# Cross-attention layer: attention stage from f32r pairs to scaled f16 pairs, and the first query tile's mask added by TensorE

## The chip, the cores and the metric

The kernel runs on one core of a Trainium2 chip. The metric is the device time of one execution in microseconds. In the views PE is TensorE (PEld its weight loads), DVE VectorE, ACT ScalarE, POOL GpSimd, and SP the engine that issues most DMAs.

## The reference

A transformer layer over 16 sequences of 512 tokens and 512 features: cross attention with 16 heads of 32, queries from `x`, keys and values from a context, then a feed-forward block of 2048.

```python
q, k, v = heads(query @ Wq + bq), heads(key @ Wk + bk), heads(values @ Wv + bv)
scores = einsum('bhqd,bhkd->bhqk', q, k) / sqrt(32)
scores = where(j < i, scores, -1e30)            # strictly causal
attn = softmax(scores); attn[:, :, 0, :] = 0
x = layer_norm(query + (attn @ v) @ Wo + bo, g1, b1_)
out = layer_norm(x + relu(x @ W1 + b1) @ W2 + b2, g2, b2_)
```

Inputs, weights and the result are f32, and the result has to keep nearly f32 accuracy. So every operand of TensorE is held as a high part and a low part (the rest), and each product is made of three matmuls: high by high, high by low, low by high.

## The kernel before

There are two stages: attention over 16 items (the sequences), and feed over 32 chunks of 256 tokens (output projection, both norms, the feed-forward block in f16 pairs). Attention writes its heads' outputs to memory (`ctx_rows`), feed reads them.

**Slots.** Each engine's program is a loop over windows, each of 48 slots. `due(window, slot, SLOTS, items, first, span)` says which items have their step `first + k` in this slot; a step number over 47 belongs to the next windows, so three items are in work at once. Within a slot each engine does what is due in the order in which it is written, and waits on semaphores for the others. All step numbers are constants at the top of `attention`. `side_by_side` mixes feed's program into attention's from slot 48 x 16 + `FEED_AFTER` on, one step of feed to two slots.

**Steps of an item.** Pieces of the context and of x (four each, 128 x 512) are loaded into the one buffer `raw` (`CTX_LOAD` 14, `X_LOAD` 27), split by ACT (high part, f32r, L459) and DVE (low part, L524) into `acts`. From `LIN` = 32 on, PE makes 12 projection units (`UNITS`: four of v, and k and q for each of four head groups), each of four slots with three matmuls (L720, L724). Of a v unit ACT and DVE take three bf16 parts out of PSUM: L476, L644 (rest into `vf`), L481, L649. Of a k or q unit they take a high and a low f32r part into `stage` (L491, L658). When a group's q is staged, SP issues 12 DMAs (`heads_moves`, L360) that lay its heads' high and low parts out as 96 rows in `heads`; each moves 128 KB.
From `MAX_AT` = 57 on, one group in 12 slots, PE makes the scores for the row maxima (L699, 11 units of a group, `MAX_UNITS`), into two banks of `max_ps`; DVE adds the mask and takes the maximum in one pass for each head (L678). The negated maxima, two parts, are transposed (L629) and moved by SP into rows 96 and 97 of `heads` (L398, four DMAs). From `ST_AT` = 74 on PE makes the transposed scores with the maximum subtracted (L746) and adds masks by a matmul with an identity (L781); ACT takes two exponentials (f32 and f16, L514, L516), POOL the low part (L435), and PE multiplies with V three slots later (L766 high, 97 columns; L768 low, 65). DVE sums the three parts of V (L599), inverts the row sum (L602) and scales (L610); SP stores the group (L389, L390).
PE in slot s may start a unit of max scores when DVE has read the unit two slots before (`max_read`).

**Beside it.** Each item also loads a piece of W1 or W2 into `raw`, and DVE looks for its largest magnitude (L582); for W2 POOL mixes blocks (L451) and SP stores them (L337). From these bounds feed's f16 scales are made.

**Start and end.** At the start v's weights and the first context come in turn, and each piece is split as soon as it is there (`first_split`, L463 and L529). Where attention's last item drains, feed's weights are split into f16 pairs in memory that attention has left, each with a wait for what was there (`before.*`).

## Time and profile before

| | |
|---|---|
| median of three runs | 2659.24 us (2656.49 to 2664.09) |
| profiled execution, span | 2657.7 us (its own time outside the span is not given; the median is 1.5 us above) |
| busy share of PE, PEld, DVE, ACT, POOL | 98%, 84%, 79%, 58%, 60% |
| chain that ended last, by engine | PE 87%, DVE 4%, SP's queue 2%, POOL 2%, DMA 2%, ACT 1% |
| DMA | 273.35 MB, mean 103 GB/s; `heads<-stage` 748 issues of 128 KB |

Shares of busy time are averages over both stages. A matmul's duration holds its way through the array, and consecutive ones overlap, so their rate is read from start to start. A time of a group by form is the mean of one instruction; starts of back-to-back DVE instructions lie somewhat closer.

### The profile page before, as it was taken

The page shows a single profiled execution, that of the slowest core. Times are in us where ns is not written, and L with a number is a line of the kernel's source. Part 1 is how long each engine was busy: PE and PEld are TensorE (multiplying, and loading weights), DVE is VectorE, ACT ScalarE, POOL GpSimd, SP SyncE. Part 2 cuts the span into 40 slices and gives each one's busy share as a digit, 9 for nine tenths or more (in the row PEclk, how much of TensorE's full clock was granted, in tenths as well). Part 3 has the DMA queues.
Part 4 walks back from the last instruction along what each step waited for, and adds up shares of the span by engine and source line. Part 5 has one row for each costly group of instructions (what it writes and reads, how often), then busy time and mean ns, then how long its engine had stood idle before and what let it go on. Part 6 is the DMA issues. An engine that isn't in the chain of part 4 may idle for free.

```text
span 2657.7 us, 62252 instructions
## 1 busy us (share of the span) xinstructions
PE 2605.2 (98%) x22600; PEld 2245.5 (84%) x22600; DVE 2088.3 (79%) x5171; ACT 1530.3 (58%) x2945; POOL 1587.9 (60%) x1721
## 2 busy tenths in 40 slices
PE   7999999999999999988999999999999999999998
PEld 5888888888888888867888888888888888888887
DVE  6888988888888888888767766676767676767675
ACT  4777877787777777766343434343434344444433
POOL 3777777766666666666555555454555555555543
PEclk9999999999999999989999999999999999999999
DMA  6566655565556555656131323222222222222220
GB/s 189 154 154 163 157 152 155 145 166 143 143 145 152 144 142 138 147 140 171 48 67 47 70 50 69 52 66 55 59 62 56 64 57 64 57 65 57 64 55 27
DMA packets 439556, 273.35 MB, mean 103 GB/s; under 512 B 299648, under 2 KB 334400, under 8 KB 439248
## 3 DMA queue, kind: packets, MB, share of 16 engines
q1 hardware_dynamic: 437648, 266.74, 40.3%
q10 hardware_dynamic: 1600, 2.62, 0.5%
q8 instruction: 178, 2.92, 0.5%
q14 instruction: 130, 1.06, 0.1%
HBM read 109.86 MB, written 57.67 MB: 63 GB/s over the span
## 4 chain that ended last, share of the span: by engine, by line
PE 87%; DVE 4%; SPq 2%; issue 2%; POOL 2%; DMA 2%; ACT 1%; ACTq 0%; DVEq 0%; POOLq 0%
PE h_ps L1443 23%; PE acc L1459 20%; PE lin_ps L724 12%; PE lin_ps L720 6%; PE front L1429 6%; PE max_ps L699 6%; PE st_ps L746 6%; PE o_ps L766 4%; PE o_ps L768 3%; PE st_ps L781 2%; POOL prob_lo L435 1%; SPq L866 1%; SPq L360 1%; DVE W L1400 1%; DMA x_in<-in_x 0%
## 5 line engine op out<-in xcount | busy, mean ns | idle before, releaser
L435 POOL TENSOR_TENSOR prob_lo<-probs,prob_hi 128x512 f16<-128x512 f32 (+1 forms) x768 | 785.1, 1035 | 369.2 <-ACT prob_hi L516 365.1
L1443 PE MATMUL h_ps<-x_halves,W 128*128 128x256 f16 x6144 | 757.2, 273 | 3.1 <-ACT hf L1234 1.7
L1443 PEld LDWEIGHTS h_ps<-x_halves,W 128*128 128x128 f16 x6144 | 596.9, 98 | 89.6 <-issue 12.0
L1459 PE MATMUL acc<-W,hs 128*128 128x256 f16 x5376 | 669.6, 273 | 0.0
L1234 ACT ACTIVATE hf<-h_ps,b1s,scale_evac 128x256 f32<-128x256 f32 x512 | 284.7, 562 | 530.5 <-PE h_ps L1443 530.1
L678 DVE CUSTOM_DVE_ANT_0 max_ps<-max_ps,mask_q 128x128 f32<-128x128 f32 (+3 forms) x1024 | 486.2, 506 | 123.6 <-PE max_ps L699 107.6
L1459 PEld LDWEIGHTS acc<-W,hs 128*128 128x128 f16 x5376 | 526.0, 98 | 60.8
L514 ACT ACTIVATE probs<-st_ps 128x512 f32<-128x512 f32 (+1 forms) x768 | 406.4, 529 | 240.5 <-PE st_ps L781 221.2
L1158 POOL TENSOR_TENSOR hf<-hf 128x256 f32<-128x256 f32 x256 | 248.5, 971 | 462.1 <-ACT hf L1234 462.0
L1396 DVE TENSOR_TENSOR hs<-hf,hs 128x896 f16<-128x896 f32 x256 | 286.9, 1141 | 157.4 <-ACT hs L1223 157.3
L516 ACT ACTIVATE prob_hi<-st_ps 128x512 f16<-128x512 f32 (+1 forms) x768 | 406.7, 530 | 0.0
L1223 ACT ACTIVATE hs<-hf 128x896 f16<-128x896 f32 x256 | 242.2, 946 | 272.6 <-POOL hf L1161 269.4
L746 PE MATMUL st_ps<-heads 98*128 98x512 f32 (+3 forms) x1024 | 310.1, 344 | 2.3 <-DMA heads<-rows 2.1
L699 PE MATMUL max_ps<-heads 96*128 96x128 f32 (+3 forms) x1024 | 279.7, 325 | 8.5 <-DVE maxima L678 6.9
L766 PE MATMUL o_ps<-V,prob_hi 128*128 128x97 bf16 x2560 | 242.9, 208 | 9.8 <-DVE onorm L610 8.5
L1159 POOL TENSOR_TENSOR hf<-hf 128x256 f32<-128x256 f32 x256 | 237.7, 929 | 0.0
L768 PE MATMUL o_ps<-V,prob_lo 128*128 128x65 bf16 x2560 | 237.5, 193 | 0.0
L720 PE MATMUL lin_ps<-wv,ctxT 128*128 128x512 f32 x768 | 226.8, 406 | 6.4 <-DVE ctxT L529 6.4
L699 PEld LDWEIGHTS max_ps<-heads 96*128 96x128 f32 x1024 | 184.8, 191 | 56.9 <-DVE maxima L678 15.9
L724 PE MATMUL lin_ps<-xT,wq 128*128 128x512 f32 x768 | 227.3, 405 | 3.4 <-DVE vf L644 2.6
L724 PE MATMUL lin_ps<-ctxT,wk 128*128 128x512 f32 x768 | 220.2, 396 | 0.0
L766 PEld LDWEIGHTS o_ps<-V,prob_hi 128*128 128x128 f16 x2560 | 210.2, 98 | 11.1 <-DVE onorm L610 9.9
(121 smaller groups left out, 3797.4 us busy)
## 6 DMA issues: line engine op xcount, KB each, us to landing
heads<-stage SPq DMA_DIRECT2D x748, 128.0 KB, 2.6
raw<-in_xT SPq DMA_DIRECT2D x64, 256.0 KB, 3.0
o_in<-ctx_rows SPq DMA_DIRECT2D x256, 64.0 KB, 2.6
x_in<-in_x SPq DMA_DIRECT2D x32, 512.0 KB, 4.1
x_rows<-x SPq DMA_DIRECT2D x64, 256.0 KB, 2.0
o_in<-x_rows SPq DMA_DIRECT2D x256, 64.0 KB, 2.4
out<-y SPq DMA_DIRECT2D x32, 512.0 KB, 3.1
raw<-in_cT SPq DMA_DIRECT2D x60, 256.0 KB, 3.5
```

The lines of the kernel that those rows point to most:

```text
L435: pool.tensor_tensor(prob_lo[:, k % 4, 0:w], probs[:, k % PROBS, 0:w], prob_hi[:, k % 4, 0:w], ALU.subtract).then_inc(pl_done, 1)
L514: act.activation(probs[:, k % PROBS, 0:w], st_ps[:, k % 2, 0:w], ACT.Exp, bias=PROB_BIAS, scale=SCALE)
L516: act.activation(prob_hi[:, k % 4, 0:w], st_ps[:, k % 2, 0:w], ACT.Exp, bias=PROB_BIAS, scale=SCALE).then_inc(exp_done, 1)
L678: last = dve.tensor_tensor_reduce(out=scores[:, a, :], in0=scores[:, a, :], in1=mask, scale=1.0, scalar=MASKED, op0=ALU.add, op1=ALU.max, ...
L699: last = pe.matmul(max_ps[:, bank, a * w:(a + 1) * w], heads[0:96, t, 0, i, q * P:(q + 1) * P], heads[0:96, t, 1, i, 0:w], start=(a == 0), ...
L720: last = pe.matmul(lin_ps[:, n % 2, :], a[:, aw, j, t * P:(t + 1) * P], W[kind][:, aa, j, :], start=(j == 0 and m == 0), stop=(j == KT - 1 ...
L724: last = pe.matmul(lin_ps[:, n % 2, :], W[kind][:, aw, j, t * P:(t + 1) * P], a[:, aa, j, :], start=(j == 0 and m == 0), stop=(j == KT - 1 ...
L746: last = pe.matmul(st_ps[:, k % 2, at:at + w], heads[0:98, t, 1, i, kt * P:(kt + 1) * P], heads[0:98, t, 0, i, kt * P:S], start=(opens and ...
L766: pe.matmul(o[:, 0:3 * HD + 1], prob_hi[:, k % 4, col:col + P], v[:, 0:3 * HD + 1], start=(k % 3 == 0 and q == 0), stop=False, skip_group_ ...
L768: last = pe.matmul(o[:, HD:3 * HD + 1], prob_lo[:, k % 4, col:col + P], v[:, HD:3 * HD + 1], start=False, stop=(c == 2), skip_group_check= ...
L1443: last = pe.matmul(h_ps[:, f % 2, 0:T], W1[:, aw, j, f * P:(f + 1) * P], x1_halves[:, item.parity, aa, j, :], start=(j == 0 and m == 0), s ...
L1459: last = pe.matmul(acc_products[:, n, :], hs[:, p % HS, aa, n, :], W2[:, p, aw, n, :], start=(p == 0 and m == 0 and n % 2 == 0), stop=(p = ...
```

## The change

All of attention's TensorE operands become pairs of f16, as in feed. f16 has a small range, so each operand is multiplied by a power of two that the kernel finds on the chip. For every item DVE looks at both halves of c and of x for the largest magnitude per partition (four reductions over 1024 elements), joins them, SP writes them to memory (`SPREAD`) and reads them back into every partition (`GATHER`), and DVE makes from them the exponent, its inverse, the scaled biases, the exponential's scale and the values' scale (`ranges`, `RANGE`). The splits multiply by the inverse. The weights and the first item get the same at the start (`first_look`, `first_join`, `first_ranges`), in two groups: c, v and k first, then x and q; no weight and no piece is split before its group's range is known. V has two f16 parts in place of three bf16 parts. The raw pieces of c, of x and of the scanned weights get buffers of their own, and `acts` becomes double. In the max scores of the first query tile the mask is added by a fifth matmul, and DVE takes one reduction over all four heads. Steps move: `LIN` from 32 to 40 and all that hangs on it, loads and splits too, `FEED_AFTER` from 30 to 38. The places in memory are laid out anew, and with them the waits of feed for what attention leaves.

```diff
+    LOAD = {"c": 0, "x": 8}
+    LOOK = {"c": 5, "x": 13}
+    TOPS = 16
+    SPREAD = 17
+    GATHER = 20
+    RANGE = 24
+    SPLIT = {"c": 28, "x": 40}
+    SPLIT_STEP = 3
+    LIN = 40
...
+        acts = sb("acts", [P, 2, 2, 2, KT, S], F16)
+        raw = {"c": sb("raw_c", [P, KT, S], F32), "x": sb("raw_x", [P, KT, S], F32)}
+        W = {w: sb(f"w{w}", [P, 2, KT, D], F16) for w in WEIGHTS}
+        stage = sb("stage", [P, 2, 2, 2, S], F16)
+        scan = sb("scan", [P, KT, D], F32)
+        heads_at = sb("heads", [P, GROUPS, 2, 4, S], F16)
...
+        V = sb("V", [P, 2, QT, HEADS, VW], F16)
...
+                for kind in KINDS:
+                    for j in range(KT):
+                        for item, _ in after_first(due(window, s, SLOTS, B, LOAD[kind] + j)):
+                            wait_for(sp, lo_done, NCHUNK, item, chunk_of(kind, j) + 1 - NCHUNK)
+                            load(kind, item, j)
...
+                for item, _ in after_first(due(window, s, SLOTS, B, SPREAD)):
+                    wait_for(sp, top_ready, 1, item, 0)
+                    sp.dma_start(top_rows, top[:, :]).then_inc(top_spread, 16)
+                for item, _ in after_first(due(window, s, SLOTS, B, GATHER)):
+                    wait_for(sp, top_spread, 16, item, 0)
+                    wait_for(sp, range_step, RANGE_STEPS, item, 1 - 2 * RANGE_STEPS)
+                    sp.dma_start(gathered[:, 0:P, :].rearrange("p r k -> p (r k)"),
+                                 top_rows.rearrange("p k -> (p k)").rearrange("(a n) -> a n", a=1)
+                                 .to_broadcast([P, 2 * P])).then_inc(top_gathered, 16)
...
+            wait_for(act, raw_loaded[kind][j], 16, item, 16)
+            act.wait_ge(*ranged(item, 3))
+            act.activation(act_part(item, kind, 0)[:, j, :], raw[kind][:, j, :], ACT.Copy,
+                           scale=inverse[:, item.n % 3, KINDS.index(kind):KINDS.index(kind) + 1]).then_inc(hi_done, 1)
...
+            dve.scalar_tensor_tensor(out=act_part(item, kind, 1)[:, j, :], in0=raw[kind][:, j, :],
+                                     scalar=inverse[:, item.n % 3, i:i + 1], in1=act_part(item, kind, 0)[:, j, :],
+                                     op0=ALU.mult, op1=ALU.subtract).then_inc(lo_done, 1)
...
+                            for j in (2 * half, 2 * half + 1):
+                                wait_for(dve, raw_loaded[kind][j], 16, item, 16)
+                            wait_for(dve, top_ready, 1, item, -1)
+                            dve.tensor_reduce(top_parts[:, KINDS.index(kind), half:half + 1],
+                                              raw[kind][:, 2 * half:2 * half + 2, :].rearrange("p i n -> p (i n)"),
+                                              AX_X, ALU.max, apply_absolute_value=True).then_inc(top_seen, 1)
...
+            wait_for(dve, top_gathered, 16, item, 0)
+            dve.tensor_reduce(tops[:, :], gathered[:, :, :].rearrange("p r k -> p k r"), AX_X, ALU.max
+                              ).then_inc(range_step, 1)
+            dve.tensor_scalar(power[:, at, :].bitcast(U32), tops[:, :].bitcast(U32), EXPONENT, None, ALU.bitwise_and
+                              ).then_inc(range_step, 1)
+            dve.reciprocal(inverse[:, at, :], power[:, at, :]).then_inc(range_step, 1)
...
+        first_join(0, 7)
+        for half in range(2):
+            first_look(1, 0, half, raw_loaded["x"][2 * half:2 * half + 2], raw["x"])
+            first_look(1, 1, half, first_loaded["q"][2 * half:2 * half + 2], first[:, 2, :, :])
+        first_ranges(0)
+        first_join(1, 5)
+        for w, j in FIRST_TURN:
+            if w == "c":
+                split(Item(0), "c", j)
+            else:
+                split_weight(w, j)
+        first_ranges(1)
...
+                            dve.tensor_tensor(V[:, item.parity, t, :, 0:HD],
+                                              lin_ps[:, n % 2, :].rearrange("p (h d) -> p h d", d=HD),
+                                              V[:, item.parity, t, :, HD:2 * HD], ALU.subtract
+                                              ).then_inc(lin_out, 1)
...
-                                          o[:, :, 0:3 * HD].rearrange("p q (c d) -> p q d c", c=3),
+                                          o[:, :, 0:2 * HD].rearrange("p q (c d) -> p q d c", c=2),
...
+                            if q == 0:
+                                dve.tensor_reduce(maxima[:, t % 2, 0, :], scores, AX_X, ALU.max
+                                                  ).then_inc(max_read, 1)
+                                continue
...
+            if q == 0:
+                last = pe.matmul(max_ps[:, bank, :].rearrange("p (h n) -> p h n", n=P), identb[:, :],
+                                 mask_q0[:, :].unsqueeze(1).to_broadcast([P, 4, P]), start=False, stop=True,
...
-                        pe.matmul(o[:, 0:3 * HD + 1], prob_hi[:, k % 4, col:col + P], v[:, 0:3 * HD + 1],
+                        pe.matmul(o[:, 0:2 * HD + 1], prob_hi[:, k % 4, col:col + P], v[:, 0:2 * HD + 1],
...
-                        last = pe.matmul(o[:, HD:3 * HD + 1], prob_lo[:, k % 4, col:col + P],
-                                         v[:, HD:3 * HD + 1], start=False, stop=(c == 2),
+                        last = pe.matmul(o[:, HD:2 * HD + 1], prob_lo[:, k % 4, col:col + P],
+                                         v[:, HD:2 * HD + 1], start=False, stop=(c == 2),
```

## Rows read from the trace of the kernel before

**Rows 1.** Busy time by window: stretch, length, engines' busy us (instructions), clock, DMA share, GB/s.

```profile
300.00:1000.00 700.00, 698.98 (x6346) 593.00 (x6345) 621.77 (x2117) 554.32 (x1191) 497.69 (x496) 1.00 0.59 149
...
1150.00:1200.00 50.00, 40.91 (x317) 32.43 (x317) 44.52 (x99) 36.05 (x73) 32.87 (x29) 0.90 0.44 120
...
1400.00:2600.00 1200.00, 1199.90 (x10265) 1054.09 (x10264) 859.38 (x1400) 498.44 (x805) 640.45 (x750) 1.00 0.26 59
```

**Rows 2.** Waits, 300 to 1000 us: total us, times, longest.

```profile
DVE max_ps L678 <- PE max_ps L699: 64.5, 128, 1.7
...
PEld max_ps L699 <- DVE maxima L678: 4.8, 11, 0.5
```

**Rows 3.** Groups by form, 300 to 1000 us, PE projections: busy us, mean ns, idle.

```profile
L720 PE MATMUL lin_ps<-wv,ctxT 128*128 128x512 f32 x480 | 139.9, 399 | 0.0
```

**Rows 4.** PE in order of time: start us, us, instruction.

```profile
640.63 0.21 PE L766 MATMUL o_ps<-V,prob_hi 128*128 128x97 bf16 x1
640.68 0.19 PE L768 MATMUL o_ps<-V,prob_lo 128*128 128x65 bf16 x1
640.71 0.21 PE L766 MATMUL o_ps<-V,prob_hi 128*128 128x97 bf16 x1
...
641.23 0.27 PE L781 MATMUL st_ps<-mask_k,identb 128*128 128x256 bf16 x1
```

**Rows 5.** Chain of waits, 1090 to 1260 us: start us, us, what.

```profile
1122.55 0.70 PE lin_ps L724 x3
...
1254.63 1.31 PE acc L1459 x12
```

**Rows 6.** Groups by form, 300 to 1000 us, weight loads.

```profile
L766 PEld LDWEIGHTS o_ps<-V,prob_hi 128*128 128x128 f16 x1586 | 129.0, 97 | 0.1
...
L699 PEld LDWEIGHTS max_ps<-heads 96*128 96x128 f32 x633 | 113.2, 189 | 29.2 <-DVE maxima L678 4.8
```

**Rows 7.** Groups by form, 300 to 1000 us, DVE.

```profile
L599 DVE TENSOR_REDUCE osum<-o_ps 128x128 f32<-128x384 f32 x159 | 87.7, 552 | 0.0
...
L649 DVE TENSOR_TENSOR V<-vf,V 128x512 bf16<-128x512 f32 x40 | 41.1, 1028 | 0.0
...
L524 DVE TENSOR_TENSOR xT<-raw,xT 128x512 fp32r<-128x512 f32 x40 | 36.9, 922 | 0.0
...
L582 DVE TENSOR_REDUCE scan_part<-raw 128x1 f32<-128x1024 f32 x10 | 12.1, 1214 | 0.0
...
L588 DVE TENSOR_TENSOR scan_top<-scan_top,scan_part 128x1 f32<-128x1 f32 x10 | 1.9, 189 | 0.3
```

**Rows 8.** Groups by form, 1400 to 2600 us, DVE.

```profile
L1321 DVE SCALAR_TENSOR_TENSOR x_halves<-block_turned,scale,x_halves 128x512 f16<-128x512 f32 x54 | 53.4, 988 | 61.5 <-ACT x_halves L1187 61.5
```

**Rows 9.** DVE in order of time, first query tile of a group.

```profile
651.92 0.30 DVE L678 CUSTOM_DVE_ANT_0 max_ps<-max_ps,mask_q 128x128 f32<-128x128 f32 x1
...
652.91 0.44 DVE L678 CUSTOM_DVE_ANT_0 max_ps<-max_ps,mask_q 128x256 f32<-128x256 f32 x1
```

**Rows 10.** SP's queue in order of time.

```profile
618.03 2.66 SPq L398 DMA_DIRECT2D heads<-rows  x4
...
636.24 0.41 SPq L350 DMA_DIRECT2D raw<-in_xT  x1
636.75 7.85 SPq L360 DMA_DIRECT2D heads<-stage  x12
```

**Rows 11.** DMA issues, 300 to 1000 us: count, KB, median us to landing.

```profile
raw<-in_xT SPq DMA_DIRECT2D x40, 256.0 KB, 3.0
```

**Rows 12.** Busy time by window, at the start.

```profile
4.00:8.00 4.00, 2.25 (x5) 1.38 (x6) 2.77 (x4) 2.31 (x4) 4.00 (x1) 1.00 0.97 354
```

**Rows 13.** All engines in order of time, at the start.

```profile
4.03 0.69 DVE L529 TENSOR_TENSOR wv<-first,wv 128x512 fp32r<-128x512 f32 x1 [4.03 <-ACT wv L463]
...
13.70 0.68 DVE L644 TENSOR_TENSOR vf<-lin_ps,V 128x512 f32<-128x512 f32 x1
```

549 lines of the change are left out of this document (337 added, 212 removed).

## The prediction

> **What bounds the kernel now.** I read the windows by stage first, then who waits for whom, then groups by form, then single stretches in order of time. The windows [rows 1] show two stages. In 300 to 1000 us, the middle of the attention stage, PE is busy for 698.98 of 700 us at the full granted clock, DVE for 621.77, ACT 554.32, POOL 497.69. In 1400 to 2600 us, the feed stage, PE is busy 1199.90 of 1200 us. Between them, at 1150 to 1200 us, PE leaves 9 of 50 us idle and its granted clock is 0.90. The waits of the attention stretch [rows 2] run one way: DVE waits 64.5 us for PE's max scores, PE waits 4.8 us for DVE. So PE sets the pace, and the question is who is second. 480 value matmuls fall in the 700 us [rows 3] and a sequence has 48 of them: one sequence takes 70.0 us. In these 70.0 us DVE works 62.2, ACT 55.4, POOL 49.8. DVE has 7.8 us of slack, and that is all that a faster PE can win before DVE binds.
>
> **PE, per sequence.** In order of time [rows 4] the 16 value matmuls from 640.63 to the mask at 641.23 take 0.60 us, so a pair (97 and 65 columns) takes 75 ns: from the first to the second 0.05, back 0.03. Three projection matmuls of 512 columns take 0.70 us [rows 5], 233 ns each. A sequence has 144 projections (33.6 us) and 160 pairs (12.0 us). The rest, 24.4 us, is 64 max-score and 64 transposed-score matmuls (20480 columns each) and 48 masks (8192 columns).
> The rate of f16 operands stands in the feed stage: 12 matmuls of 256 columns in 1.31 us [rows 5], 109 ns each or 0.426 ns a column. At that rate the projections take 144 x 0.218 = 31.4 us (2.2 less), and the rest 49152 x 0.426 = 20.9 us (3.5 less). Value pairs get 65 and 33 columns. 65 is measured at 29 ns (to 30 as printed); 33 lies between its columns alone (14 ns) and the same 29. I take 29, since the fixed part of so short a matmul is not shown: 160 x 0.058 = 9.3 us, 2.7 less. The new mask matmul, 512 columns, comes four times: 0.9 us more. Sum 70.0 - 2.2 - 3.5 - 2.7 + 0.9 = 62.5 us. Lower end, with 14 ns for 33 columns: 60.1. Upper end, if the scores and masks gain nothing: 66.0.
> The Trainium skill, "TensorE: Matmul & The Clock Gate", section "Wait — 56ns, not 53.3ns?", gives a floor of about 25 ns from start to start for any short matmul. By it a pair would take 54 ns and the PE sum, as an estimate, 61.9; no row here has a matmul that short.
> Why f32 operands pay more: the weight loads take 189 ns in f32 and 97 in f16 [rows 6], the first not far from the 233 ns of a 512-column matmul beside which the next load has to pass.
>
> **DVE, per sequence** [rows 7 to 9]. Gone: the second value subtraction, L649, 41.1 us in ten sequences, 4.1. The first one (L644) stays as the only one, at its price. The three-way sum of L599 becomes two-way, 384 to 256 elements: from L582 (1024 elements, 1214 ns) and L599 (384, 552 ns) 128 elements cost 0.132 us, so 16 x 0.132 = 2.1. The first query tile's four mask-and-max steps take 0.99 us (651.92 to 652.91); one reduction over 512 elements costs 0.552 + 0.132 = 0.68: 4 x 0.31 = 1.2 less. Added: four looks over 1024 elements, one for each half of each input, 4 x 1.214 = 4.9; one small maximum and the range steps (a reduction over 258 elements 0.42, five small ones at about 0.2, as L588 takes 0.19) 1.6. The splits become a scaled subtraction with f16 out. The same form in the feed stage takes 988 ns [rows 8] against 922 now: 8 x 0.07 = 0.6 more (at best the 690 ns of the undisturbed start [rows 13], 1.9 less). Sum 62.2 - 4.1 - 2.1 - 1.2 + 6.5 + 0.6 = 61.9 us, bounds 59.4 and 63.
> The Trainium skill, "SBUF — State Buffer", section "Who interferes with whom", has it that a DVE instruction with two SBUF inputs and a GpSimd one that reads SBUF lock each other out, which fits 922 ns beside POOL's work and 690 before it began. The rule speaks against the hope that f16 makes the splits cheap: by it they stay two-input instructions, and the sum, as an estimate, stays within 0.6 us of mine.
> So DVE's load stays, and PE comes down to it: 62.5 against 61.9.
>
> **ACT and POOL.** ACT loses the third value piece (4 x about 0.6 us) and works 53. POOL keeps 49.8. Both stay below 62 and hide.
>
> **The new wait: loads behind the head moves on SP.** SP issues in program order. The moves of one head group are 12 DMAs, 7.85 us by the clock of the queue [rows 10], 0.65 each; a whole load takes 0.5 and a quartet of row moves 2.66. Halving the bytes need not shorten this, as a load of twice the bytes takes less time to issue. Per sequence SP issues 48 moves (31 us), 16 row moves (11), ten loads (5) and eight stores, which I put at 10: some 57 of 70 us. Two more small DMAs (the spread and the gather of the ranges) make 58; SP as a whole does not bind.
> The order does. The x loads stand at slots 8 to 11 and the moves of group 0 at slot 9, so pieces 2 and 3 are issued behind all 12. The moves wait for DVE's q piece of slot 8. From there 12 x 0.62 = 7.4, two issues 0.9 and 2.6 to 3.0 us to landing [rows 11] give 10.9 to 11.3 us, and 1.3 more in the first eight sequences, where the store of the mixed W2 stands between. DVE comes to the second x look (slot 15) after about 7 slots of 1.3 us with the first two x pieces in hand; its own work in them is some 7.5 us, PE's 8.5 to 9. So it waits about 2.5 us (ends 0 and 3.8). What is queued behind: DVE's whole slot 15 and all later ones, among them the max reads that free PE's two banks; PE may run two slots ahead, no more. With DVE and PE both near 62, this wait is not absorbed.
> Behind it hang the small maximum, the spread (SP, behind four row moves), 2 to 2.5 us to memory, the gather and again 2.5 us back, due on DVE at slot 24, 16 slots or 21.6 us after slot 8. The chain is 11.1 + 1.4 + 2.7 + 0.5 + 2.3 + 0.5 + 2.8 = 21.3 us: just in time. But SP stands still for the round trip at slot 20, and the group 1 moves (slot 21) start late by about a slot, against a margin of 8 slots (10.8 us) less 7.4 + 2.5 us (to landing, put a little below the load's 3.0). I put 0.7 us on both, with the unevenness of slots (ends 0 and 4).
> Sum of the new period: 61.9 + 0.4 for dependent small steps + 2.6 + 0.7 = 65.6 us, 4.4 less than now.
>
> **Start.** Now the first value piece leaves PSUM at 13.70 us [rows 13]. The change wants v, c, k and the biases looked at first. Twenty loads of 262 KB come in at 354 GB/s in 4 to 8 us and faster after [rows 12]: k is in by about 12 us, all by 17. DVE: four looks done by 11, biases and two k looks by 14.2; out to memory and back 0.5 + 2 + 0.5 + 2.5, to 19.7, with the x and q looks (4.9) beside it; 14 chained steps 3.3, to 23; eight splits of 0.69, to 28.7; the second range 3.3, to 32; the k splits 2.8, to 34.8. So 21 us later than now, nothing beside it on PE. Ends 14 and 27.
>
> **Between the stages.** The tail is paced by POOL, ACT and the feed stage's own weight splits, which keep their work; new places in memory drop a few waits for buffers and add others that are long over. I count 0, ends -8 and +6. The feed stage is untouched. The longer lead (40 slots for 32) holds no work and costs nothing.
>
> **Sum.** The pace of 70.0 us holds from 35 to 1110 us, 15.3 sequences: 15.3 x 4.4 = 67 us less; 21 more at the start: 46 less. The span of the profiled execution is 2657.7 us; 2611.7. The median of the runs is 1.5 us above that span, so 2613.
>
> **Rivals.**
> B, the look wait stays hidden: DVE's work between slots 8 and 15 is slower than I count, or the moves issue faster at half the bytes. Then PE's 62.5 sets the pace. For: raw loads issue in 0.5 us with twice the bytes; against: the moves' 0.65 us is steady whatever the traffic. 15.3 x 7.5 = 115 less, 21 more: 2565. Chance 0.25.
> C, SP's order takes the place of PE (the slower side): the x pieces late by 3.8 us with the mixed store, the ranges late at slot 24 by 1.5, the group 1 moves behind SP's standstill late by 2 at slot 29, on a DVE of 63. Period 70.3: 5 more and 21 more: 2685. It decides from a period of 68.6 on (15.3 x 1.4 = 21). For: SP is busy 57 of 70 us and waits now at DVE's q piece; against: all three must come in full. Chance 0.16.
> D, the change doesn't speed PE as it says: max and transposed scores keep their 24.4 us, as their time is in turn-around between differently shaped weights and not in f32. PE 66.0, with the looks partly beside it 67: 46 less, 21 more: 2634. For: 24.4 is 3.5 over the columns' 20.9 and I have f16 only in even streams; against: 189 ns loads. Chance 0.14.
> The forecast's own case, 2613, has 0.45, with 2590 to 2640 as its own range. Range over all: 2560 to 2662. A measurement tells 0.3%, 8 us, from no change: faster 0.79 (the forecast, B, most of D), same 0.06, slower 0.15.
>
> **What would show it.** Per sequence, by the count of value matmuls: 65.6 us; DVE busy over 92% of the stretch, PE near 95%, and PE's waits for DVE's max reads in tens of us where there were 4.8. The looks on x with a wait for a raw x load of 2 to 3 us, 15 times. Projections at 218 ns, value pairs at 58. First value piece out of PSUM near 35 us. Wrong: PE still busy 99.8% with a period near 62 (B), a wait of the PE for head moves (C), score matmuls at their old spacing (D), or a first value piece before 28 us.

## The result, and the profile after

| | before | after |
|---|---|---|
| median | 2658.74 us (2656.49 to 2664.09, four runs) | 2820.3 us (2815.91 to 2822.85, four runs) |
| ratio after/before, 95% interval | | 1.0605 [1.0589, 1.062] |
| span of the profiled execution | 2657.7 us | 2817.5 us |
| first value matmul of item 0 | 5.8 us | 27.2 us |
| from item 0's to item 1's | 59.5 us | 60.4 us |
| fourteen periods, items 1 to 15 | 988.1 us, 70.6 each | 1128.2 us, 80.6 each |
| from item 15's first value matmul to the end | 1604.3 us | 1601.7 us |

The change makes the kernel 6% slower, 207 us above the forecast of 2613 us. The last four rows are worked out from the trace: 48 projection matmuls of an item belong to the values, so the start of each 48th marks where an item begins on PE. They add up to the whole difference of the spans: 21.4 + 0.9 + 140.1 - 2.6 = 159.8 us. The start cost what was forecast (21.4 + 0.9, for 21), the passage between the stages about nothing (-2.6, for 0), and all of the miss lies in the period: 80.6 us where 65.6 was forecast. It isn't one number either. While the scan still mixes and stores W2 (items 1 to 7) a period is 81.8 to 84.1 us, afterwards 76.5 to 79.5.

Page of the kernel after, parts 1 and 4: busy time by engine, and the chain that ended last.

```profile
PE 2553.5 (91%) x22664; PEld 1903.7 (68%) x22664; DVE 2122.2 (75%) x4871; ACT 1628.7 (58%) x2881; POOL 1579.7 (56%) x1721
...
PE 53%; issue 11%; POOL 10%; DVE 10%; SPq 9%; DMA 6%; ACT 1%; POOLq 0%; DVEq 0%; ACTq 0%
```

The chain was 87% PE before. Now PE has 53% of it, nearly all in the feed stage, and the rest is spread over everything: issue, POOL, DVE, SP's queue, DMA. That is the picture of a loop in which no engine is full. The windows say the same (columns as in [rows 1]):

```profile
0.00:35.00 35.00, 7.85 (x23) 2.46 (x24) 24.05 (x55) 10.29 (x16) 12.16 (x20) 1.00 0.67 211
...
300.00:1000.00 700.00, 594.24 (x5613) 341.75 (x5613) 563.49 (x1686) 543.25 (x1013) 445.63 (x437) 0.94 0.35 93
...
1600.00:2700.00 1100.00, 1099.52 (x9402) 965.68 (x9400) 779.26 (x1278) 450.58 (x733) 567.85 (x688) 1.00 0.26 59
```

In the attention stretch PE is busy for 594 of 700 us where [rows 1] have 699, DVE for 563 where they have 622, and the granted clock is 0.94 where it was 1.00. The feed stage is as full as before. Times 80.6 and over 700 this is, per item: PE 68.4, DVE 64.9, ACT 62.6. None of them reaches 81.

The waits of the same stretch, a selection (total us, times, longest):

```profile
PE max_ps L905 <- DVE maxima L884: 70.7, 41, 7.5
DVE max_ps L884 <- PE max_ps L905: 63.1, 85, 1.8
PE o_ps L974 <- POOL prob_lo L493: 30.6, 40, 4.1
DVE top_parts L833 <- issue: 33.9, 5, 7.5
DVE top_parts L833 <- DMA raw_x<-in_xT: 12.3, 4, 3.4
DVE scan_part L772 <- DMA scan<-in_W: 11.0, 7, 2.1
POOL scan L508 <- DMA scan<-in_W: 20.6, 4, 5.5
DVE tops L678 <- DMA gathered<-top_rows: 4.4, 5, 2.1
```

In the kernel before, PE's weight loads waited 4.8 us for DVE's max reads [rows 2] and its matmuls not at all; the matmuls wait 70.7 us now. DVE's waits for the second x look are nine, 46.2 us by their two releasers: 5.9 to 7.5 us in each of five items, 2.4 to 3.4 in each of four later ones. Each is followed, 2 us on, by a wait of PE of the same length, which makes 46 of the 70.7 us. ("issue" here is a wait whose releaser, a DMA that landed long after it was issued, the view could not name; the timelines below show what it is.) So DVE waits for a load and PE for DVE. PE's 30.6 us for POOL's low parts have a like cause: while W2 is mixed, POOL stands for the scanned weights' load up to 5.5 us, and PE then 3.3 to 4.1 us for POOL, once an item.

One such stall in order of time. SP's queue:

```profile
445.61 0.89 SPq L352 DMA_DIRECT2D raw_x<-in_xT  x2
449.44 8.49 SPq L419 DMA_DIRECT2D heads<-stage  x12
457.98 0.58 SPq L352 DMA_DIRECT2D raw_x<-in_xT  x1
458.61 1.51 SPq L396 DMA_DIRECT2D mixed_w<-scan  x3
460.16 0.56 SPq L352 DMA_DIRECT2D raw_x<-in_xT  x1
...
467.64 2.68 SPq L456 DMA_DIRECT2D heads<-rows  x4
470.37 0.41 SPq L431 DMA_DIRECT2D top_rows<-top  x1
473.38 0.33 SPq L437 DMA_DIRECT2D gathered<-top_rows  x1
```

DVE and PE (start us, us, instruction):

```profile
455.24 1.19 DVE L833 TENSOR_REDUCE top_parts<-raw_x 128x1 f32<-128x1024 f32 x1
...
464.83 1.22 DVE L833 TENSOR_REDUCE top_parts<-raw_x 128x1 f32<-128x1024 f32 x1 [6.87 <-issue]
...
466.86 0.59 PE L905 MATMUL max_ps<-heads 96*128 96x128 f16 x4 [6.86 <-DVE maxima L884]
...
467.66 1.49 PE L932 MATMUL lin_ps<-acts,wq 128*128 128x512 f16 x3
...
470.42 0.81 PE L932 MATMUL lin_ps<-acts,wq 128*128 128x512 f16 x3
```

Windows across it:

```profile
461.00:463.00 2.00, 0.00 (x0) 0.00 (x0) 0.00 (x0) 0.00 (x0) 1.18 (x2) 1.00 1.09 396
463.00:465.00 2.00, 0.00 (x0) 0.00 (x0) 0.17 (x1) 0.00 (x0) 0.00 (x0) 0.55 0.29 108
465.00:467.00 2.00, 0.14 (x2) 0.17 (x3) 2.00 (x6) 0.00 (x0) 0.00 (x0) 0.50 0.37 114
467.00:469.00 2.00, 2.00 (x9) 0.88 (x8) 1.93 (x8) 0.00 (x0) 0.00 (x0) 0.50 0.04 11
469.00:471.00 2.00, 2.00 (x22) 1.40 (x21) 1.41 (x7) 1.07 (x3) 0.15 (x1) 0.75 0.03 3
```

The reader should follow one thing through these three views. The twelve moves of group 0 start when DVE's q piece is staged, at 449.4. Behind them SP issues a load, three stores of the mixed W2 and the last load, whose issue ends at 460.7 and which lands at 464.8, when the look starts. DVE came to the look at 458.0 and stood for 6.9 us; its max reads stood with it, PE stood for as long, and from 461 to 465 every engine but POOL is idle. PE then starts again at half the clock: the granted clock falls from 463 us on and is 0.50 at 465 to 469 us, the lower of its two levels (1.2 GHz), after PE has done nothing since 460. Three projection matmuls take 1.49 us there (at 467.66) and 0.81 us at 470.42, where the clock is back; from start to start it is 0.43 us for one against 0.22. The spread of the ranges stands behind the four row moves (2.7 us), and the gather is issued 3.0 us after the spread, as it waits for its landing: both as forecast.

What was forecast of PE's instructions came out. Value pairs and masks (columns as in [rows 4]):

```profile
477.61 0.19 PE L974 MATMUL o_ps<-V,prob_hi 128*128 128x65 f16 x1
477.64 0.18 PE L976 MATMUL o_ps<-V,prob_lo 128*128 128x33 f16 x1
...
477.94 0.22 PE L989 MATMUL st_ps<-mask_k,identb 128*128 128x128 bf16 x1
```

Six pairs in 0.33 us are 55 ns each (75 before). Starts of 512-column projections and scores lie 215 to 219 ns apart (projections 233 before), of 384 columns 165 to 166, of 256 columns 110 to 113 (medians). The mask matmul of 512 columns takes 220 ns. The Trainium skill, "TensorE: Matmul & The Clock Gate", section "Wait — 56ns, not 53.3ns?", has a floor of about 25 ns between starts; the 26 ns in which a 33-column matmul makes way for the next agree with it, where its columns alone would give 14.

Groups by form, 300 to 1000 us, a selection of those that answer to [rows 7 to 9] or are new:

```profile
L833 DVE TENSOR_REDUCE top_parts<-raw_x 128x1 f32<-128x1024 f32 x17 | 20.5, 1205 | 46.2 <-issue 33.9 <-DMA raw_x<-in_xT 12.3
L592 DVE SCALAR_TENSOR_TENSOR acts<-raw_c,inverse,acts 128x512 f16<-128x512 f32 x36 | 38.6, 1074 | 0.0
L804 DVE SCALAR_TENSOR_TENSOR onorm<-osum,value_scale,o_ps 128x128 f32<-128x128 f32 x139 | 47.4, 341 | 0.0
L790 DVE TENSOR_REDUCE osum<-o_ps 128x128 f32<-128x256 f32 x140 | 58.5, 418 | 0.0
L879 DVE TENSOR_REDUCE maxima<-max_ps 128x4 f32<-128x512 f32 x35 | 24.1, 688 | 3.1 <-PE max_ps L909 2.9 <-issue 0.2
L584 ACT ACTIVATE prob_hi<-st_ps,exp_scale 128x512 f16<-128x512 f32 x278 | 195.5, 703 | 0.0
```

The looks (1.21 forecast), the sum of two parts (0.42) and the one reduction (0.68) are at their forecast prices. Three are dearer: the splits at 1050 to 1074 ns for 988 forecast, the scaling at 341 for 280 before, and ACT's exponential at 703 ns for 598 before. The forecast had no term for the last two.

### The profile page after: what moved, and what is told of

Read it like the earlier page. It is cut to its first block, busy times and chain, and to the rows that moved or that the text cites. A ratio compares the mean times of both kernels' runs of the same rounds, so it can differ in the third digit from the quotient of the medians.

```text
span 2817.5 us, 62084 instructions
## 1 busy us (share of the span) xinstructions
PE 2553.5 (91%) x22664; PEld 1903.7 (68%) x22664; DVE 2122.2 (75%) x4871; ACT 1628.7 (58%) x2881; POOL 1579.7 (56%) x1721
## 3 DMA queue, kind: packets, MB, share of 16 engines
q14 instruction: 126, 1.03, 0.1%
## 4 chain that ended last, share of the span: by engine, by line
PE 53%; issue 11%; POOL 10%; DVE 10%; SPq 9%; DMA 6%; ACT 1%; POOLq 0%; DVEq 0%; ACTq 0%
PE h_ps L1649 22%; PE acc L1665 19%; POOL prob_lo L493 10%; SPq L419 7%; PE front L1635 6%; DVE max_ps L884 2%; PE lin_ps L932 2%; DMA scan<-in_W 1%; DMA raw_x<-in_xT 1%; DMA gathered<-top_rows 1%; SPq L456 1%; DMA top_rows<-top 1%; PE max_ps L905 1%; DVE W L1606 1%; PE st_ps L954 1%
## 5 line engine op out<-in xcount | busy, mean ns | idle before, releaser
L493 POOL TENSOR_TENSOR prob_lo<-probs,prob_hi 128x512 f16<-128x512 f32 (+1 forms) x768 | 793.3, 1043 | 461.1 <-ACT prob_hi L584 457.2
L1649 PEld LDWEIGHTS h_ps<-x_halves,W 128*128 128x128 f16 x6144 | 596.2, 98 | 90.7 <-issue 15.4
L582 ACT ACTIVATE probs<-st_ps,exp_scale 128x512 f32<-128x512 f32 (+1 forms) x768 | 482.8, 629 | 282.1 <-PE st_ps L989 231.4
L1665 PEld LDWEIGHTS acc<-W,hs 128*128 128x128 f16 x5376 | 525.9, 98 | 61.6 <-DVE hs L1602 0.8
L884 DVE CUSTOM_DVE_ANT_0 max_ps<-max_ps,mask_q 128x256 f32<-128x256 f32 (+2 forms) x768 | 420.1, 562 | 116.9 <-PE max_ps L905 115.6
L584 ACT ACTIVATE prob_hi<-st_ps,exp_scale 128x512 f16<-128x512 f32 (+1 forms) x768 | 484.1, 630 | 0.0
L905 PE MATMUL max_ps<-heads 96*128 96x128 f16 (+3 forms) x1024 | 267.0, 314 | 124.1 <-DVE maxima L884 116.0
L974 PE MATMUL o_ps<-V,prob_hi 128*128 128x65 f16 x2560 | 221.2, 193 | 77.0 <-POOL prob_lo L493 56.3
L954 PE MATMUL st_ps<-heads 98*128 98x512 f16 (+3 forms) x1024 | 275.1, 309 | 4.0 <-DMA heads<-rows 2.3
L928 PE MATMUL lin_ps<-wv,acts 128*128 128x512 f16 x768 | 211.3, 386 | 27.2 <-DVE acts L592 27.2
L932 PE MATMUL lin_ps<-acts,wq 128*128 128x512 f16 x768 | 225.9, 406 | 4.2 <-DVE V L851 4.2
L932 PE MATMUL lin_ps<-acts,wk 128*128 128x512 f16 x768 | 212.9, 387 | 3.1 <-DVE V L851 3.1
L976 PE MATMUL o_ps<-V,prob_lo 128*128 128x33 f16 x2560 | 213.1, 181 | 0.0
```

Of the source, the lines that this page charges most:

```text
L493: pool.tensor_tensor(prob_lo[:, k % 4, 0:w], probs[:, k % PROBS, 0:w], prob_hi[:, k % 4, 0:w], ALU.subtract).then_inc(pl_done, 1)
L582: act.activation(probs[:, k % PROBS, 0:w], st_ps[:, k % 2, 0:w], ACT.Exp, bias=PROB_BIAS, scale=exp_scale[:, at:at + 1])
L584: act.activation(prob_hi[:, k % 4, 0:w], st_ps[:, k % 2, 0:w], ACT.Exp, bias=PROB_BIAS, scale=exp_scale[:, at:at + 1]).then_inc(exp_done, 1)
L884: last = dve.tensor_tensor_reduce(out=scores[:, a, :], in0=scores[:, a, :], in1=mask_q[:, S - w:S], scale=1.0, scalar=MASKED, op0=ALU.add, ...
L905: last = pe.matmul(max_ps[:, bank, a * w:(a + 1) * w], heads[t][0:96, 0, i, q * P:(q + 1) * P], heads[t][0:96, 1, i, 0:w], start=(a == 0), ...
L932: last = pe.matmul(lin_ps[:, n % 2, :], W[kind][:, aw, j, t * P:(t + 1) * P], act_part(item, side, aa)[:, j, :], start=(j == 0 and m == 0) ...
```

## Experiments

A period is given as the mean of the fourteen from item 1 to item 15 (before: 70.6). E1 to E6 ask how much the wait for the loads and the search cost; E7 and E8 put parts of the f16 pairs alone into the kernel before; F and G, run afterwards, take the rest apart. The ratio is against runs of the kernel before on the same chip. The series ran on four chips, where the kernel before took 2659.5 (E1 to E4), 2657.6 (E5 to E8), 2657.9 (F) and 2657.6 us (G), so a difference of times between two series can be up to 2 us off.

**E1: the x loads before the head moves.** Only their place changes; the look, the moves and all else stay.

```diff
-    LOAD = {"c": 0, "x": 8}
+    LOAD = {"c": 0, "x": 4}
```

> The changed kernel with the x loads four slots earlier (slots 4 to 7), ahead of group 0's 12 head moves in SP's order; nothing else. Theory 1 (order): DVE's second x look waits 6.9 us (sequences with the mixed W2 store) or 3.4 us (those without) for x pieces issued behind the moves, and nothing absorbs it: the period falls from 82.5 and 78.5 us to about 76 and 75, the wait at the look goes to 0, and the time from 2820 to about 2740 us. Rival 2 (load): ACT at 62 us, DVE at 64 us per sequence and their uneven slots set the period; the wait only moves to another place: 2800 us or more.

Measured: 2775.1 us, 1.0439 [1.0423, 1.0455]. Windows, 300 to 1000 us:

```profile
300.00:1000.00 700.00, 609.01 (x5849) 350.03 (x5848) 603.85 (x1750) 564.02 (x1052) 461.63 (x454) 0.97 0.37 97
```

The waits of the x look are gone altogether, and with them 45 us. That lies between the expectation (about 2740) and its rival (2800 or more). So the mechanism was there, but it is not the main part: the periods are still 76.6 to 79.6, then 75.7 to 77.9, 77.4 in the mean. What is late next are the scan look (1 to 2 us) and the gather (up to 2.4 us).

**E2: the scan's load before the moves of group 3 as well.**

```diff
-    SCAN_LOAD = 42
+    SCAN_LOAD = 38
```

> As e1, and the scanned weights' load goes from slot 42 (behind the moves of group 3) to slot 38 (ahead of them). Theory 1: POOL's wait for this load (20.6 us in 8.75 sequences, four long ones of 5 us) and DVE's (1.4 to 2.1 us a sequence) go, and with them PE's waits for POOL's low parts (5 us a sequence in the first half): another 3 to 5 us a sequence in the first half and 1 in the second, 2740 to about 2705 us. Rival 2: no change against e1.

Measured: 2751.2 us, 1.0338 [1.0317, 1.0358]; period 75.8. The scan's load is worth 24 us, not the 35 expected. The order of loads is worth 69 us together (2820 to 2751), and 92 of the 161 us over before remain. The waits left in 300 to 1000 us, a selection (SP's from its own view):

```profile
PE max_ps L905 <- DVE maxima L884: 32.7, 40, 3.0
PE o_ps L974 <- DVE onorm L804: 30.2, 18, 2.5
SPq L437 <- DMA top_rows<-top: 25.0, 9, 3.9
DVE tops L678 <- DMA gathered<-top_rows: 12.9, 8, 2.9
```

**E3: no search after the first item.** Its range is used for all: four looks, the joining, spread, gather and ranges of each later item are left out. (The operands are scaled as before; only the finding is missing.)

```diff
-                for item, _ in after_first(due(window, s, SLOTS, B, SPREAD)):
+                for item, _ in ():
...
-                        for item, _ in after_first(due(window, s, SLOTS, B, LOOK[kind] + 2 * half)):
+                        for item, _ in ():
...
-                    at = item.n % 3
+                    at = 0
```

> The changed kernel without the search for scales after the first item: no looks, no small maximum, no spread and gather, no range steps for items 1 to 15; all items use the first item's scales (the per-item search is left out). Splits, loads and f16 arithmetic stay, the x loads stay behind the moves. Theory 1: what is lost is lost in the chain of looks and round trips; the period falls to 68 or 70 us in both halves, a little more in the first (scan load), time about 2650 to 2680. Rival 2: ACT's 62 us and the slots' unevenness keep it at 74 us or more: 2740.

Measured: 2708.0 us, 1.018 [1.0164, 1.0196]. Period 72.8: 75.7 in the mean of the first half, where the scan's load still stands behind the moves, and 70.0 in the second:

```profile
620.00:1000.00 380.00, 348.54 (x3488) 205.62 (x3487) 322.82 (x985) 336.01 (x629) 269.18 (x261) 1.00 0.38 102
```

The time lies between the expectation (2650 to 2680) and its rival (2740), and this run turned the search for the cause. Without the search DVE works 59.5 us of a period, PE 64, ACT 62, the clock is at its full level, and yet the period is 70 and not 64. Something other than the search keeps the loop from PE's pace.

**E4: the mask on PE in the kernel before.**

```diff
+            if q == 0:
+                last = pe.matmul(max_ps[:, bank, :].rearrange("p (h n) -> p h n", n=P), identb[:, :],
+                                 mask_q0[:, :].unsqueeze(1).to_broadcast([P, 4, P]), start=False, stop=True,
...
+                            if q == 0:
+                                dve.tensor_reduce(maxima[:, t % 2, 0, :], scores, AX_X, ALU.max
```

> The kernel before with one part of the change alone: the first query tile's mask added by a fifth matmul, and one reduction of DVE over four heads. PE sets the pace there: four more matmuls of about 0.22 us a sequence, 0.9 us x 15: 14 us more, about 2673 us. Rival: DVE's relief (1.2 us a sequence) outweighs it, 2659 or less.

Measured: 2669.0 us, 1.004 [1.0025, 1.0055], 9.5 us more (14 expected); a steady period is 71.2, against 70.4 before. It costs 0.8 us of PE, where the forecast put 0.9 and PE is full: DVE's 1.2 us less give nothing back.

**E5 and E6: the exponential's scale as a constant.** With this data it has the same value for every item, so nothing is left out but the read of the operand. E5 is E3 with this edit, E6 is E2 with it.

```diff
-                                   scale=exp_scale[:, at:at + 1])
+                                   scale=SCALE)
```

> e3 (first item's scales for all) with the exponential's scale as a constant in place of a value read per partition; the constant is the same number for these inputs. In e3's second half every engine has slack (PE 64.3 of 70.0 us, DVE 59.4, ACT 62.1) and still the period is 70.0. Theory 3 (ACT): an exponential with its scale read from memory takes 703 ns for 512 columns against 598, ACT's load rose from 55.8 to 62.1, and the way PE scores, ACT, POOL, PE values became too long for its three slots: with the constant ACT falls to about 55, the period to 66 or 67 in the second half, time from 2708 to about 2660. Rival 4 (slots): PE and DVE, coupled over two banks with unlike slots, hold the period; ACT's relief brings under 1 us a sequence: 2695 or more.

> e2 (x and scan loads ahead of the moves, all looks in place) with the constant scale of the exponential. Theory 3: from 75.5 us a sequence to about 72, time 2751 to about 2700. Rival 4: the looks hold DVE at 67 busy us and its lumps bind: 2735 or more. Theory 1 alone would give no change.

Measured: E5 2689.4 us, 1.0117 [1.0101, 1.0133], period 71.5, 18.6 us below E3; E6 2719.5 us, 1.0229 [1.0205, 1.0253], period 73.7, 31.8 us below E2. (With the two chips' times of before taken off, 17 and 30 us.) Each lies between its two expectations. E5, second half:

```profile
620.00:1000.00 380.00, 352.40 (x3551) 208.54 (x3550) 330.43 (x1003) 296.53 (x638) 273.32 (x265) 0.99 0.39 104
```

ACT falls from 62 to 54 us a period, and the period from 70.0 to 68.5. ACT was not full, yet its length counts. The way is probably that PE's value products wait for POOL's low part, which waits for ACT. It explains a part and not the rest: 68.5 is still 5 us over PE's work (63.6).

**E7 and E8: the pairs alone, in the kernel before, with no scales and no search.** E7 gives V two f16 parts and drops the third piece's steps; E8 makes the heads, the staged k and q and the negated maxima f16 as well. Padding keeps every other buffer at its place. With no scales these are bound to inputs that fit f16 as they are.

```diff
-        V = sb("V", [P, 2, QT, HEADS, VW], BF16)
+        V = sb("V", [P, 2, QT, HEADS, VW], F16)
...
-                        pe.matmul(o[:, 0:3 * HD + 1], prob_hi[:, k % 4, col:col + P], v[:, 0:3 * HD + 1],
+                        pe.matmul(o[:, 0:2 * HD + 1], prob_hi[:, k % 4, col:col + P], v[:, 0:2 * HD + 1],
```

```diff
-        stage = sb("stage", [P, 2, 2, 2, S], F32R)
+        stage = sb("stage", [P, 2, 2, 2, S], F16)
...
-        heads = sb("heads", [P, GROUPS, 2, 4, S], F32R)
+        heads_at = sb("heads", [P, GROUPS, 2, 2, 4, S], F16)
```

> The kernel before with one part of the change alone: V as two f16 parts instead of three bf16, without any scale (the search for scales is left out, these inputs need none). PE is the pace there: a value pair falls from 75 to 55 ns, 160 pairs: 3.2 us a sequence less, period 70.4 to 67.2, time 2659 to about 2611. DVE loses 6 us, ACT 2.5, no new wait. Rival 4: slots take part of it: period 69, time 2640.

> e7 and the heads' pairs (both score matmuls, the head moves, the negated maxima) in f16, again without scales; projections and inputs stay f32r, no looks, loads at their old places. PE: 128 score matmuls lose what f32 weights cost, 3.5 us a sequence; period 63.7 if PE goes on setting it, time about 2560. Rival 4 (slots): PE's slack of a few us shows up as waits at the max reads, period 66 to 67, time 2600.

Measured: E7 2626.8 us, 0.989 [0.9875, 0.9905], period 68.5, PE 67.8 of it; E8 2594.9 us, 0.9763 [0.9748, 0.9777], period 66.9, PE 65.4. Both parts are real gains of PE. Its work falls from 70.5 by 2.7 and then by 2.4, for 2.7 and 3.5 forecast, and the period by 2.1 and 1.6: PE begins to have gaps. In both the slower expectation (2640 and 2600) is the nearer one.

**F1: looks without ranges.** E2 with the looks and their joining, without spread, gather and ranges for each item. It tells the load of DVE from the round trips.

```diff
-                for item, _ in after_first(due(window, s, SLOTS, B, GATHER)):
+                for item, _ in ():
...
-                for item, _ in after_first(due(window, s, SLOTS, B, RANGE)):
+                for item, _ in ():
```

> e2 (x and scan loads ahead of the moves, 75.5 us a sequence) with DVE's looks and their small maximum kept, and the spread, the gather and the range steps left out; all items use the first item's scales. Theory 5 (load): the looks' 5 us on DVE, in pieces of 1.2 us beside a two-bank lead, are what costs: period 74, time 2735. Theory 6 (round trip): SP standing still for the spread's landing and DVE waiting for the gather (2 to 3 us) cost the more: period 71, time 2685.

Measured: 2708.5 us, 1.0182 [1.0165, 1.02]; period 73.0. It fell between the two expectations: the round trips and ranges cost 2.8 us a period (75.8 to 73.0), the looks 3.9 (below, F2).

**F2: no search, loads early.** E3 with the load slots of E2: what the after's schedule and layout can do with nothing searched.

```diff
-    LOAD = {"c": 0, "x": 8}
+    LOAD = {"c": 0, "x": 4}
...
-    SCAN_LOAD = 42
+    SCAN_LOAD = 38
```

> e3 (no search for scales after the first item) with the x and scan loads ahead of the moves: the floor of this layout with the exponential's scale read from memory. In the second half e3 has 70.0 us: 69.0 to 69.5 expected here in both halves, PE's clock at 1.00; time about 2670 (e3: 2708). If the mixing of W2 blocks on POOL is what costs e3's first half (75.3 us), the first half stays at 73 or more.

Measured (ten runs): 2653.5 us, 0.9981 [0.9971, 0.999]; period 69.1, nearly the same in both halves (expected were 2670 us and 69.0 to 69.5). As the first half doesn't stay at 73, it is the late load of the scan and not the mixing that costs E3 its first half. Windows and a selection of the waits, 300 to 1000 us:

```profile
300.00:1000.00 700.00, 652.84 (x6522) 386.38 (x6519) 600.69 (x1839) 628.43 (x1177) 520.91 (x506) 1.00 0.40 107
```

```profile
PE o_ps L972 <- POOL prob_lo L491: 19.2, 43, 0.7
PE o_ps L972 <- DVE onorm L802: 14.4, 10, 1.7
PE max_ps L903 <- DVE maxima L882: 8.0, 17, 0.5
DVE max_ps L882 <- PE max_ps L903: 80.2, 121, 2.3
```

The difference between F1 and F2: the four looks of an item cost 3.9 us of period (69.1 to 73.0) for 4.8 us of DVE's time, though DVE has 9.8 us to spare in each of F2's periods. And even here PE is 7% idle: 43 and 17 waits of under 0.75 us for POOL and for DVE's max reads, and ten of up to 1.7 us for DVE's scaling. With the four engines loaded between 51 and 64 of 69 us, no one of them can be called the bound.

**F3, F4, G1: the search in smaller lumps, and off SP.** F3 is E2 with eight looks of 512 elements for four of 1024, those of x from one slot earlier on (12 for 13). F4 is E2 with the spread and the gather issued from ACT's queue. G1 has both.

```diff
-                    for half in range(2):
-                        for item, _ in after_first(due(window, s, SLOTS, B, LOOK[kind] + 2 * half)):
+                    for j in range(KT):
+                        for item, _ in after_first(due(window, s, SLOTS, B, LOOK[kind] + j)):
```

```diff
-                    sp.dma_start(top_rows, top[:, :]).then_inc(top_spread, 16)
...
+                    act.dma_start(top_rows, top[:, :]).then_inc(top_spread, 16)
```

> e2 with each look split in two: eight reductions over 512 elements in eight slots, in place of four over 1024. DVE's load rises by 0.5 us. Theory 5 in the form that the lumps count: period falls by 1 to 1.5 us, 2751 to about 2730. If the load alone counts: 2755 to 2760.

> e2 with the spread and the gather issued by ACT instead of SP, same slots. SP no longer stands still at slot 20, and the trips don't wait for SP's row moves. Theory 6: the wait for the gather goes, group 1 moves start on time, 2 us a sequence: 2751 to about 2720. Theory 5: under 1 us a sequence, 2740 or more. ACT's queue may be held for part of a slot by the landing, which would eat some of it.

> The whole change with all three cures: x and scan loads ahead of the moves (e2), spread and gather on ACT's queue (f4), looks in quarters (f3). If the shares add: 2820 - 69 (loads) - 20 (trips) - 17 (quarters) = about 2714 us, period 73. If trips and quarters hide each other: 2730. Not below 2690, the looks' load (f1 against f2: 55 us) stays.

Measured: F3 2734.6 us, 1.0285 [1.0269, 1.03]; F4 2731.7 us, 1.0275 [1.0259, 1.029]; G1 2720.4 us, 1.0235 [1.0218, 1.0252]; periods 74.8, 74.4 and 73.7. Against E2 these are 17, 20 and 31 us less (15, 18 and 29 with the chips' times of before taken off), so in G1 the two cures hide each other in part. A look of 1.2 us in one slot costs more than two of 0.67 in two slots, although the eight together take 5.4 us and the four 4.8. With F4 DVE's wait for the gather is gone and SP no longer stands still for it; ACT now does, 10.3 us in four waits.

**G2: all pairs in f16, old slots, no search.** E8 with the projections' operands in f16 as well, so all of PE's gain without the scales. Bound to the same inputs as E8.

```diff
-        W = {w: sb(f"w{w}", [P, 2, KT, D], F32R) for w in "vkq"}
+        W_at = {w: sb(f"w{w}", [P, 2, 2, KT, D], F16) for w in "vkq"}
+        W = {w: a[:, 0, :, :, :] for w, a in W_at.items()}
```

> e8 with the projections' operands (x, context, the three weights) in f16 pairs too, without scales and so without any search (left out), on the slots and load places of the kernel before. PE's account: projections from 233 to 218 ns, 2.2 us a sequence: period 66.6 to 64.5 or 65, time about 2565. If the slots bind at 66 us (PE 65.4 busy of 66.6 in e8 with small waits at the max reads): 2590.

Measured: 2566.9 us, 0.9657 [0.9643, 0.9672], period 65.0, as expected (about 2565). It is the fastest version, for inputs whose range is known to fit.

```profile
300.00:900.00 600.00, 578.79 (x5898) 345.99 (x5897) 533.31 (x1936) 495.07 (x1073) 457.74 (x458) 0.99 0.41 113
```

PE's work is 62.6 us of a period. The forecast of PE alone (62.5 with the mask, which is not in G2, so 61.6) was right to 1 us. The other 2.4 us of the period are gaps: in the 600 us PE waits 13.2 us for the moves of the negated maxima (`heads<-rows`), 4.0 for DVE's max reads.

**G3: the kernel before with the exponential's scale from memory.** A constant column, filled once; same value, same everything.

```diff
-                                   scale=SCALE)
+                                   scale=bounds.exp_scale[:, :])
```

> The kernel before with the exponentials' scale read per partition from SBUF instead of a constant (same value). Theory 3: each 512-column exponential goes from 598 to about 700 ns, ACT from 55.8 to 64 or 65 us of 70.4; with PE at 100% the period moves little, 0 to 0.5 us: 2659 to 2666. Rival 7: at 64 us ACT is already late for PE's three-slot lead in some slots: 1 us a sequence or more, 2675.

Measured: 2658.6 us, 1.0001 [0.9992, 1.0011]. Groups by form, 300 to 1000 us:

```profile
L520 ACT ACTIVATE prob_hi<-st_ps,exp_scale 128x512 f16<-128x512 f32 x318 | 219.9, 691 | 0.0
```

The exponential takes 691 ns for 598 with nothing else changed, which shows that the scale operand is the cause. ACT has 8 us more per item, and the time is the same: where PE is full, PE hides it. In E3 and E2, where PE has gaps, taking it away was worth 17 and 30 us. The same cost is nothing in one kernel and 0.6 to 1.1% in others.

## Why the prediction was wrong, point by point

The mean period, as one thing after another is added:

| kernel | what it has | period, us | step |
|---|---|---|---|
| before | f32r and bf16 parts | 70.6 | |
| G2 | all f16, old slots, no scales, no search | 65.0 | -5.6 |
| F2 | scales, mask on PE, new slots and places | 69.1 | +4.1 |
| F1 | and four looks | 73.0 | +3.9 |
| E2 | and spread, gather, ranges | 75.8 | +2.8 |
| after | and x and scan loads behind head moves | 80.6 | +4.8 |

Each step is the difference of two kernels in this order and would be another in another order: the late loads cost 4.8 with the search (E2 to after) and 3.7 without it (F2 to E3).

The forecast's period was 65.6, about where the ladder starts. The step that failed is the sum "61.9 + 0.4 + 2.6 + 0.7 = 65.6 us", and behind it the sentence "So DVE's load stays, and PE comes down to it: 62.5 against 61.9": the period was taken as the busiest engine's work plus the few waits that I had named. Piece by piece:

1. *The pace as a maximum.* F2 has no search and no late load, and no engine works over 64.4 us; by the forecast's rule its period would be PE's 62.5, and it is 69.1. Even G2's is 2.4 over its busiest engine. My reading of this is argued and not shown by a run of its own: PE may run only two slots ahead of DVE, its value products follow POOL, POOL follows ACT, and each slot's longest link counts, which is not always the same one. With one engine at 99.9%, as in [rows 1], the others' unevenness is hidden behind it, as G3 shows for ACT. Of the 4.1 us from G2 to F2 about 1.3 are the exponential's scale (72.8 to 71.5, E3 to E5). The other 2.8 lie in the mask's 0.8, dearer splits and scaling, and the moved slots and places; I did not separate these, and this stays open.
2. *"ACT loses the third value piece (4 x about 0.6 us) and works 53."* and *"Both stay below 62 and hide."* ACT works 62 us. I had priced what ACT lost and not what its kept instructions became: 105 ns more for each 512-column exponential, 95 for each of 256, 100 for each split. The change names the exponential's scale among what DVE makes, so it could be seen that it would no longer be a constant; the forecast gave ACT no term for it.
3. *"Added: four looks over 1024 elements, one for each half of each input, 4 x 1.214 = 4.9"*. The DVE time was right (1.205 us each), its effect was not. It was set off against V's pieces and sums that went, as if only DVE's total counted. Four lumps of 1.2 us in slots of 1.4 to 1.5 us cost 3.9 us of period beside an engine that has 9.8 to spare (F1 against F2), and halving them to 512 elements gives 15 to 17 us of time back (F3). DVE's total was too low as well: it works 64.9 us a period (66.2 in E2), over the forecast's upper bound of 63. The scaling's price (16 x 0.06 = 1.0 us) had no term, the range steps and the small maximum take 2.1 us for 1.6, and the pace before was 70.4 to 70.6 by the starts of its value matmuls, not the 70.0 that a count over 700 us gave.
4. *"So it waits about 2.5 us (ends 0 and 3.8)."* The place and the mechanism were right, and E1 took the wait away by the cause named. The size was not: 5.3 to 7.5 us in the eight items up to 631 us (6.9 in the one above) and 2.4 to 4.1 in the seven after. From the q piece to the look lie 15.4 us: 8.5 of moves, 0.6, 1.5 of mixed stores, 0.6, and 4.1 to landing, for 7.4 + 0.9 + 1.3 + 3.0 = 12.6 forecast at most. DVE arrived after 8.5 us, a time that I took as 7.5 to 9. The landing was taken too short: 3.0 is the median of 40 loads in traffic of 149 GB/s on average, and this one is issued right behind the three mixed stores and lands in traffic of 396 GB/s (window 461 to 463).
5. *Missing: the scan's load.* It also stands behind twelve moves, of group 3. DVE waits 1 to 2 us and POOL up to 5.5 for it in each item of the first half. The forecast counted SP's order for x alone. Taking the wait away was worth 24 us (E1 to E2).
6. *"I put 0.7 us on both"*, the round trip and its standstill of SP: 2.8 us a period (F1 to E2, with the range steps' own 2.0 us on DVE in it). F4 gives 1.4 a period of it to SP's queue.
7. *Missing: the clock.* After 6.9 us of idling from 460 on, PE is granted half the clock at 465 to 469, and until about 469.7 its matmuls start at twice their distance, some 1.4 us more (an estimate, half of 466.9 to 469.7). Over the stretch the clock is 0.94, in E1 and E2 0.97, in F2 1.00, and PE's busy time for one item goes with it: 68.4, 67.4, 66.7 and 64.4 us. How much of these 4 us reaches the period, no run told apart; it is inside the steps of the table.

Rival C was the right kind, "SP's order takes the place of PE", and had the right sign, but its three parts made 70.3 where 80.6 came: it was built on the same sum. Its point of decision, 68.6, was passed by F2 already, without any of its three parts. B and D are refuted: PE is not busy 99.8%, and scores do speed up (512 columns in 219 ns; PE's work 2.4 us less from E7 to E8, for 3.5 forecast).

What was right: PE's account (G2: 62.6 of work for 61.6; projections 215 ns for 218, pairs 55 for 58; E4: mask 0.8 for 0.9); the head moves' issue time with half the bytes (0.64 us, as before, so that SP gained nothing); the start; the passage between the stages. In the start the first value matmul comes 21.4 us later and item 1's 22.3, for 21 forecast, but that is in part luck. The way out to memory and back takes 8.3 us (13.25 to 21.57) where 5.5 was put, and the range steps are shorter; the first value piece leaves PSUM on DVE at 37.8 us, 24.1 later than before, where about 35 was forecast:

```profile
10.65 2.38 DVE L606 TENSOR_REDUCE first_part<-first 128x1 f32<-128x1024 f32 x2
...
13.25 0.33 SPq L371 DMA_DIRECT2D first_out<-first_top  x1
...
21.57 1.05 DVE L625 TENSOR_REDUCE first_range<-first_rows_in 128x4 f32<-128x512 f32 x1 [2.68 <-DMA first_rows_in<-first_out]
...
27.15 8.35 PE L928 MATMUL lin_ps<-wv,acts 128*128 128x512 f16 x24 [27.15 <-DVE acts L592]
```

The range was too narrow on its slow side (2662) for a reason that can be named: every rival took the period as the busiest engine's work plus named waits, so that none held the case in which no engine is full.

## What to carry to other kernels

When one engine is full, the profile says little of how well the others fit together. Before a change relieves it, count per slot and not per item, and put a price on the case that no engine becomes the new bound (in F2 the period is 4.7 us over the busiest engine's work, with three engines over 85% loaded). Look at the kept instructions as closely as at the added and removed ones: a constant that became an operand in memory changed 768 pairs of exponentials. And follow every load that stands behind a burst of moves in the same queue, with landing times taken from the moment of the burst.

## What the runs showed of the hardware that was not expected

- ACT's exponential over 512 elements takes 598 ns with a constant scale and 691 to 703 with one per partition from memory (256 elements: 390 and 485; a split copy: 634 to 646 and 740). The addition is about 100 ns in each of these. G3 shows it for the exponential alone.
- A DMA of the head moves takes SP 0.64 us to issue whether it carries 128 or 64 KB. Its landing fell from 2.6 to 2.1 us (medians), and the whole traffic from 273 to 225 MB.
- Two of the range steps' smallest instructions take 616 and 508 ns in the mean (the exponents of two numbers per partition, L681, and the exponential's scale, L685), beside 149 and 166 for the others of that size. It isn't their own work. In the 15 items L681 takes 0.17 us three times and 0.28 to 1.01 us twelve times, and in these twelve it starts while POOL's low part (L493) runs and ends 23 to 30 ns after it; L685 takes 0.20 us the three times when POOL does nothing beside it, and 0.43 to 0.61 otherwise. POOL and DVE at such a place (start us, us, instruction):

```profile
957.70 1.15 POOL L493 TENSOR_TENSOR prob_lo<-probs,prob_hi 128x512 f16<-128x512 f32 x1 [0.49 <-ACT prob_hi L584]
957.86 1.01 DVE L681 TENSOR_SCALAR power<-tops 128x2 uint32<-128x2 uint32 x1
```

- The splits get no cheaper by f16: 999 and 909 ns in G2, whose splits have no scale, for 922 and 899 before. The prediction's 690 ns of the start is not a time without POOL: [rows 12] have POOL busy for 4.00 of 4.00 us there, with one memset, which reads nothing.
